# One-hot counting kernel on Trainium2: samples dealt to the partition halves by twelves, count matmuls that write every fourth run of three columns, evictions in runs of twelve

## The reference

```python
x = mlp(dense_x, bottom)                                      # 13 -> 512 -> 256 -> 64, relu
pooled = vmap(lambda tab, ix: take(tab, ix, axis=0).sum(axis=1))(tables, indices)   # (26, 2048, 64)
Tcat = concatenate([x[:, None, :], transpose(pooled, (1, 0, 2))], axis=1)           # (2048, 27, 64)
Z = einsum('bim,bjm->bij', Tcat, Tcat)
R = concatenate([x, Z[:, li, lj]], axis=1)                    # lower triangle: 351 products
y = mlp(R, top)                                               # 415 -> 512 -> 256 -> 1, sigmoid at the end
```

## Time and profile before

| | |
|---|---|
| median of 3 runs | 2874.72 us |
| the profiled execution | 2880.54 us |
| its span, first to last instruction | 2878.7 us |
| TensorE matmul busy | 2756.6 us (96%) |
| ScalarE busy | 2113.8 us (73%) |
| VectorE busy | 1995.2 us (69%) |
| GpSimd busy | 1805.9 us (63%) |
| DMA, mean over the span | 58 GB/s |

### The profile page before, as it was taken

How to read it: one execution, slowest core, us unless ns; L and a number is a source line. 1 busy time by engine, 2 the same in 40 slices (tenths; PEclk the granted TensorE clock), 3 DMA queues, 4 the chain that set the end, 5 groups by cost and what they waited for, 6 DMA issues and landing times.

```text
span 2878.7 us, 65596 instructions
## 1 busy us (share of the span) xinstructions
PE 2756.6 (96%) x24204; PEld 1309.0 (45%) x24204; DVE 1995.2 (69%) x3358; ACT 2113.8 (73%) x2496; POOL 1805.9 (63%) x1640
## 2 busy tenths in 40 slices
PE   5999999999999999999999999999999999999798
PEld 2344444444444444444444444444444444448574
DVE  4477787877878778787777877778777778734121
ACT  2678878788787787877878878788787887853232
POOL 3277777777777777777777777777777777200000
PEclk8999999999999999999999999999999999996668
DMA  2112122121221212212122121121221212118611
GB/s 69 62 32 76 31 76 74 32 76 30 76 74 32 76 29 77 75 30 76 42 64 76 31 78 55 49 77 29 78 73 33 76 29 76 31 29 129 119 31 31
DMA packets 173102, 167.99 MB, mean 58 GB/s; under 512 B 116104, under 2 KB 134328, under 8 KB 167476
## 3 DMA queue, kind: packets, MB, share of 16 engines
q1 hardware_dynamic: 121380, 110.94, 13.8%
q0 software_dynamic: 51200, 52.53, 8.0%
q10 hardware_dynamic: 272, 0.52, 0.1%
HBM read 143.83 MB, written 20.05 MB: 57 GB/s over the span
## 4 chain that ended last, share of the span: by engine, by line
PE 82%; ACT 11%; issue 3%; SPq 1%; DMA 1%; ACTq 1%; DVE 1%; DVEq 0%; POOL 0%; POOLq 0%
PE ps L693 58%; PE ps L674 14%; ACT counts L841 6%; PE ps L637 5%; PE ps L766 4%; ACT parts L803 4%; ACT parts L810 1%; SPq L509 0%; ACT h_bot L854 0%; DMA pooled<-pooled_sb 0%; ACTq L838 0%; SPq L532 0%; DMA look_in<-in_r_indices 0%; DMA products<-zt 0%; SPq L516 0%
## 5 line engine op out<-in xcount | busy, mean ns | idle before, releaser
L611 POOL DMA_INDIRECT rows<-in_L_rec_tables,look x1600 | 1788.8, 1118 | 622.9 <-issue 453.1
L841 ACT CAST counts<-ps 128x792 int32<-128x792 f32 (+1 forms) x1848 | 1712.3, 984 | 476.2 <-PE ps L674 463.5
L693 PE MATMUL ps<-counts,parts 128*128 128x512 fp8e3 x8232 | 2024.3, 389 | 0.0
L693 PEld LDWEIGHTS ps<-counts,parts 128*128 128x128 f16 x8232 | 719.2, 96 | 914.8 <-issue 11.5
L1058 DVE TENSOR_TENSOR onehot_p<-iota_by_unit,place 128x1024 bf16<-128x1024 bf16 x924 | 638.5, 691 | 395.4 <-PE ps L674 367.3
L674 PEld LDWEIGHTS ps<-onehot_c,onehot_p 60*128 60x128 bf16 x14448 | 370.5, 95 | 482.3 <-ACT counts L841 276.3
L674 PE MATMUL ps<-onehot_c,onehot_p 60*128 60x99 bf16 x14448 | 522.7, 208 | 56.1 <-ACT counts L841 39.2
L1063 DVE TENSOR_TENSOR onehot_c<-column_c,weighted_s 128x792 bf16<-128x792 bf16 x924 | 521.4, 564 | 0.0
L1019 DVE SCALAR_TENSOR_TENSOR raw<-raw,coef_next,parts 128x896 f32<-128x896 f32 x147 | 169.1, 1150 | 59.7 <-ACT parts L803 59.7
L1092 DVE TENSOR_REDUCE rows<-rows 128x64 f32<-128x384 f32 (+1 forms) x240 | 189.9, 791 | 13.9 <-DVE pooled_sb L1069 13.9
L394 DVE COPY zt<-ps 32x208 f32<-32x208 f32 x128 | 64.8, 507 | 151.0 <-PE ps L766 149.1
(11 more groups left out here) (82 smaller groups left out, 529.3 us busy)
## 6 DMA issues: line engine op xcount, KB each, us to landing
raw<-in_L_rec_tables SPq DMA_DIRECT2D x21, 1792.0 KB
raw<-in_L_rec_tables SPq DMA_DIRECT2D x21, 1344.0 KB
rows<-in_L_rec_tables,look POOLq DMA_INDIRECT x1600
pooled<-pooled_sb SPq DMA_DIRECT2D x84, 128.0 KB
slots<-pooled SPq DMA_DIRECT2D x30, 352.0 KB, 7.9
products<-zt SPq DMA_DIRECT2D x16, 351.0 KB
idx_raw<-in_r_indices SPq DMA_DIRECT2D x42, 79.7 KB
gathered<-bags_t SPq DMA_DIRECT2D x42, 64.0 KB
```

What stands on the lines that cost most here:

```text
L611: nc.gpsimd.indirect_dma_start(rows[:, s, l, :], None, rows_flat, bass.IndirectOffsetOnAxis(ap=look[:, c, s * PL + l:s * PL + l + 1].bitca ...
L693: mm = nc.tensor.matmul(acc[k % 2][:, 0:NB], parts[:, j, :], count_bytes[k % 2][:, j % COLS, 0:NB, j // COLS], start=(j == 0), stop=(j == ...
L841: nc.scalar.copy(counts[k % 2][:, :, u * UG * GS:(u * UG + g) * GS].rearrange("p c (g h s) -> p h g c s", h=HALVES, s=HS), unit_ps[unit_bu ...
```

## The change

Three things are changed together.

The first 12 samples of a unit now stand in the lower half of the partitions and the next 12 in the upper half, where they alternated by threes. For that `load_indices` takes each half and each of the four groups of a unit in a DMA of its own: 8 DMAs, one for the whole groups of the last unit, and one for its tail, instead of 3. The last unit, of 8 samples, now lies in the lower half alone, in 3 groups, where it was 2 groups in both halves; the upper half of its groups is counted all the same, and not evicted. There are 87 groups in a block instead of 86.

A count matmul writes its 33x3 results with a step: run c of three goes to PSUM column 12c + 3x, where x is the group in its unit. It wrote 99 adjacent PSUM columns.

The eviction reads the same 2x396 numbers in order, and writes each of the 33 columns in runs of 12 int32 for each half instead of runs of 3. The last unit's eviction still has 396 numbers.

```diff
-    GROUPS = -(-NB // GS)
-    TAIL = NB - (GROUPS - 1) * GS
     UG = 4
+    US = UG * GS
+    UH = UG * HS
+    UNITS = -(-NB // US)
+    WHOLE = (UNITS - 1) * UG
+    LAST = NB - (UNITS - 1) * US
+    LAST_GROUPS = -(-LAST // HS)
+    GROUPS = WHOLE + LAST_GROUPS
+    TAIL = LAST - (LAST_GROUPS - 1) * HS
...
-                cut = (GROUPS - 1) * GK
+                cut = (UNITS - 1) * US * L
                 for h in range(HALVES):
-                    sp.dma_start(idx_raw[0:GROUPS - 1, :, h * HP:h * HP + HK],
-                                 flat[:, 0:cut].rearrange("k (g h r) -> h g k r", h=HALVES, r=HK)[h]
-                                 ).then_inc(idx_loaded, 16)
+                    for x in range(UG):
+                        sp.dma_start(idx_raw[x:WHOLE:UG, :, h * HP:h * HP + HK],
+                                     flat[:, 0:cut].rearrange("k (u h x r) -> h x u k r", h=HALVES, x=UG, r=HK)[h, x]
+                                     ).then_inc(idx_loaded, 16)
...
-                        last = nc.tensor.matmul(unit_ps[unit_buffer(k, u)][:, h, x * HC:(x + 1) * HC],
+                        last = nc.tensor.matmul(unit_ps[unit_buffer(k, u)][:, h, :].rearrange(
+                            "p (c x s) -> p x c s", x=UG, s=HS)[:, x, :, :],
...
-                act.wait_ge(idx_loaded, 48 * t + 48)
+                act.wait_ge(idx_loaded, 160 * t + 160)
...
-                g = len(units_of(u))
+                halves = HALVES if u < UNITS - 1 else 1
                 nc.scalar.copy(
-                    counts[k % 2][:, :, u * UG * GS:(u * UG + g) * GS].rearrange(
-                        "p c (g h s) -> p h g c s", h=HALVES, s=HS),
-                    unit_ps[unit_buffer(k, u)][:, :, 0:g * HC].rearrange("p h (g c s) -> p h g c s", c=COLS, s=HS),
+                    counts[k % 2][:, :, u * US:u * US + halves * UH].rearrange("p c (h b) -> p h c b", b=UH),
+                    unit_ps[unit_buffer(k, u)][:, 0:halves, :].rearrange("p h (c b) -> p h c b", b=UH),
                 ).then_inc(counts_ready, 1)
```

More of the change, by code:

```diff
@@ L66, in build @@
     BLOCKS = B // NB
-    GROUPS = -(-NB // GS)
-    TAIL = NB - (GROUPS - 1) * GS
     UG = 4
+    US = UG * GS
[6 more added lines that the diff above has]
+    TAIL = LAST - (LAST_GROUPS - 1) * HS
+    assert LAST <= UH
     LG = 2
     SUBS = UG // LG
-    UNITS = -(-GROUPS // UG)
     PAIRS = UNITS // 2
-    BPAD = GROUPS * GS
+    BPAD = (UNITS - 1) * US + UH
     CHUNKS = 7
@@ L430, in load_indices @@
                 flat = indices[t].rearrange("b l -> (b l)").rearrange("(k r) -> k r", k=BLOCKS)
-                cut = (GROUPS - 1) * GK
+                cut = (UNITS - 1) * US * L
                 for h in range(HALVES):
-                    sp.dma_start(idx_raw[0:GROUPS - 1, :, h * HP:h * HP + HK],
-                                 flat[:, 0:cut].rearrange("k (g h r) -> h g k r", h=HALVES, r=HK)[h]
-                                 ).then_inc(idx_loaded, 16)
+                    for x in range(UG):
+                        sp.dma_start(idx_raw[x:WHOLE:UG, :, h * HP:h * HP + HK],
+                                     flat[:, 0:cut].rearrange("k (u h x r) -> h x u k r", h=HALVES, x=UG, r=HK)[h, x]
+                                     ).then_inc(idx_loaded, 16)
+                full = (LAST_GROUPS - 1) * HK
+                sp.dma_start(idx_raw[WHOLE:GROUPS - 1, :, 0:HK],
+                             flat[:, cut:cut + full].rearrange("k (g r) -> g k r", r=HK)).then_inc(idx_loaded, 16)
                 sp.dma_start(idx_raw[GROUPS - 1:GROUPS, :, 0:TAIL * L],
-                             flat[:, cut:NB * L].rearrange("k (g r) -> g k r", g=1)).then_inc(idx_loaded, 16)
+                             flat[:, cut + full:NB * L].rearrange("k (g r) -> g k r", g=1)).then_inc(idx_loaded, 16)
             def load_lookups(n):
@@ L813, in convert_indices @@
             def convert_indices(t):
-                act.wait_ge(idx_loaded, 48 * t + 48)
+                act.wait_ge(idx_loaded, 160 * t + 160)
                 nc.scalar.copy(idx_f[:, :, 0:TAIL * L], idx_raw[:, :, 0:TAIL * L]).then_inc(idx_converted, 1)
-                for cols in (slice(TAIL * L, HK), slice(HP, HP + HK)):
-                    nc.scalar.copy(idx_f[0:GROUPS - 1, :, cols], idx_raw[0:GROUPS - 1, :, cols]
-                                   ).then_inc(idx_converted, 1)
+                for groups, cols in ((GROUPS - 1, slice(TAIL * L, HK)), (WHOLE, slice(HP, HP + HK))):
+                    nc.scalar.copy(idx_f[0:groups, :, cols], idx_raw[0:groups, :, cols]).then_inc(idx_converted, 1)
             def copy_bags(n):
```

## The result

The changed kernel takes 3038.2 us (median of 4 runs, 3032.02 to 3041.5) against 2875.66 us before; the ratio, taken over all the runs and not from the two medians, is 1.0557, 95% interval 1.0533 to 1.0582. It is slower, as forecast, but by 163 us instead of 50, and lies above the range. The profiled execution took 3037.09 us, 157 us more than the one of before.

A forecast was written before the change was run, and what follows sets the result against it. TensorE was taken to set the pace, ScalarE for about a tenth of the span. 2880.5 + 87 (stepped writes, added pair) + 3 (start) - 40 = 2930.5, less 5.8 above the median: 2925 us, range 2838 to 2955.

The forecast's parts named there:

- Evictions: ScalarE's copies out of PSUM: writing runs of twelve instead of three saves 0.11 us on each of 792 numbers.
- The line through copies of 256 and 896 numbers: ScalarE copies writing adjacent numbers, 0.89 ns a number: gives 893 ns for an eviction of 792 numbers.
- The step: Count matmuls' stepped PSUM writes on TensorE: 0.09 us more for 8 pairs; with the added pair, 87 us in all.
- ScalarE's 0.41 ns a run: Price ScalarE pays for a break in its output, used to size the stepped writes of count matmuls.
- The sum of these steps: Whole kernel: 2880.5 + 87 + 3 - 40 = 2930.5 us, forecast 2925 us since the profiled execution stood above the median.
- ScalarE's full stretch: Block counting the next table's first block, where ScalarE works without pause and TensorE loses time: 28 us freed wholly.
- the turn: Turn of the round, where TensorE waits: shorter wait saves 8 us, fewer rounds at half clock 4 us.
- the step costs nothing: Rival: count matmuls' stepped writes are free and evictions faster; 2849 us, range 2838 to 2862, chance 0.36.
- The start: Kernel's beginning: seven more DMA issues at 0.42 us each add 3 us, bounds 0 and 6 us.
- VectorE's index work on 348 instead of 344 columns: nothing: VectorE's index work in the loop: the added columns cost nothing.
- the whole matmul at half rate: Rival: stepped count matmuls write wholly at half rate, 256 us more instead of 87, about 3095 us; chance 0.05.

The follow-up runs named there:

- the even stride: Changed kernel with 88 instead of 87 index columns a block, so every slice of place starts at an even element: 2922.68 us, ratio 1.0164.
- the odd stride alone: Kernel before with 87 instead of 86 index columns a block, nothing else changed: 3036.39 us, ratio 1.0554.
- the odd rows: Kernel of twelves without the step, with place one column wider so only its row 1 starts at an odd element: 2930.91 us, ratio 1.0199.
- twelves without the step: Changed kernel with 88 index columns and count matmuls writing adjacent columns; the eviction gathers runs of three from PSUM: 2850.13 us, ratio 0.9911.

## Why the prediction was right and wrong

**Evictions: right in direction, too small.** The forecast took 0.11 us of saving; it is 0.18 (1002 to 823). The line through copies of 256 and 896 numbers, 893 ns at 792, was no lower end. For 198 runs fewer that is 0.90 ns a run, twice the 0.41 of the forecast. (The excess of the two forms over that line, 109 ns for 264 runs and 65 for 132, was not in proportion to their runs either: 0.41 and 0.49 ns.) The rule of 16-byte lines (the Trainium skill, SBUF — State Buffer, "Door 1: The DMA port swizzle") agrees in kind: runs of twelve fill whole lines. It names no price.

**The step: right, by luck in its size.** The forecast took 0.09 us a group of 16 and a block of 29.6; measured are 0.08 and 29.51. The rule of PSUM's lines of two float32 (the Trainium skill, Advanced Engine Details and Errata, "PSUM Cachelines") agrees: 99 single columns cost nearly two columns each. The rows alone had given the same size, but from ScalarE's 0.41 ns a run, which came out at 0.90; with that, the same working would have made the step some 0.2 us a group.

**The sum of these steps: right, and its terms in part not.** With the even stride the kernel takes 2922.68 us; the forecast was 2925. The 40 us taken off in the sum were 28 for ScalarE's full stretch and 12 at the turn. By the mean length of blocks, the kernel with the even stride gets back about 21 us in the first and 22 us at the turn; its count matmuls waited 39.2 us for evictions before and wait 1.7 us now. The errors cancel, among them that of the start. The rival "the step costs nothing" gave 2849 us, and the kernel in which it costs nothing, since there is none, takes 2850.13.

**The start: too small.** Seven loads more cost more than 3 us. In the kernel without the step SyncE's eight quarter loads take 0.84 us each to issue, not 0.42, and the mlp at the start begins 7.5 us later; 5.6 of these are left at the end of the first block (151.4 against 145.8).

**The step that failed** is the sentence "VectorE's index work on 348 instead of 344 columns: nothing". I counted the columns' work, and not where the slices begin. 87 is odd. The one-hot comparison takes 1.2 us instead of 0.69 at an odd start (shown by the even stride and the odd stride alone; the odd rows show the same for `column_c`), and this costs 115.5 us on top of the rest. The second half of the same fault is that VectorE, at 69% busy, and GpSimd, at 63%, were taken to have room. GpSimd's gathers fill 114 of a round's 119 us when the time between them is counted, and they get longer when VectorE's operations do. Where the operand starts at an odd element, 80 gathers and the mean round are the same length:

| kernel | mean gather, us | 80 of them with 0.30 us between, us | mean round, us |
|---|---|---|---|
| before | 1.118 | 114 | 118.8 |
| twelves without the step | 1.150 | 116 | 117.0 |
| the step, even stride | 1.153 | 116 | 120.5 |
| odd rows | 1.212 | 121 | 121.1 |
| changed | 1.274 | 126 | 126.0 |
| odd stride alone | 1.279 | 126 | 126.4 |

None of the rivals held this; the one nearest in time, the whole matmul at half rate (3095 us), is refuted by the runs of 3 at 0.57 us.

**What is shown and what isn't.** That the odd start makes the comparison slow, and that the step costs one column for each of its odd runs, is shown by runs. That most of the loss goes through the gathers is shown by the traces: the table above, the chain with 23% of the span in L621, and VectorE's 125 us of waiting; the run with a fifth of the gathers fits it. Why a gather gets longer is shown as far as this: in the changed kernel's trace 210 gathers begin while VectorE does a reduction, which reads one SBUF tile, and 58 while it adds a PSUM tile to an SBUF tile (L1078); none of them takes over 0.97 us. Of 306 that begin beside an idle VectorE, one does. Of 551 that begin beside the one-hot comparison, which reads two SBUF tiles, 463 take over 1.00 us, and the mean is 1.52. Reading two tiles isn't quite the whole of it: of five that begin beside a conversion of one tile (L965), four take about 1.05 us.

The Trainium skill (SBUF — State Buffer, "Who interferes with whom") says that a VectorE instruction with two SBUF inputs contends with a GpSimd instruction that reads SBUF, and the trace agrees with these counts. The same section infers that generating a DMA's descriptors needs the write side alone, which such a VectorE instruction leaves free; the gathers of up to 4.00 us across comparisons speak against that. That it is the shared port is argued: no run changed the port.

## What to carry to other kernels

When a change shifts a size that sets where slices begin, work out the start of every slice in bytes, on each engine that reads it: a count that goes from even to odd can cost more than the change was about. Before calling an engine free, add its time between instructions to its busy time over one round, and ask what lengthens its instructions. Here it paid to let the engine that reads PSUM reorder, and to let TensorE write adjacent columns (2850 against 2923 us).

## What the runs showed of the hardware

- A bfloat16 comparison of two SBUF tiles on VectorE (128x1024) takes 0.69 us with all slices at even elements, 1.21 us with the broadcast one at an odd element; 128x2904 takes 1.67 and 3.18 us. The first is 1.75 times, the second 1.90 times as long.
- A matmul of 99 columns pays about one more column for each run of its output, all of odd length here: 0.49, 0.52, 0.57 and 0.79 us for 16 of them, two at a time, with 1, 11, 33 and 99 runs.
- A ScalarE eviction of 792 numbers writes runs of twelve int32 in 823 ns and runs of three in 1002 ns; whether it reads PSUM in order or in runs of three makes no difference (823 both).
- An indirect gather on GpSimd takes 0.94 us while VectorE is idle or does a reduction, and up to 4.00 us across its comparisons of 1.22 us, which read two SBUF tiles.
- Two prices that end in the same wait don't add: the odd stride costs 162 us in the kernel before, and 115.5 us in the one with the stepped writes.
